# Column totals and a bank of inverses in the cross stage of a decoder layer

## The reference, cut to what matters

```python
sn = rmsnorm(slots, slot_norm_w)
scores = einsum('bkd,bmd->bkm', sn @ Wq.T, k_proj) * SCALE
attn = softmax(scores, axis=-2)                      # over the slots k
attn = attn / (sum(attn, axis=-1, keepdims=True) + EPS)   # over the context rows m
updates = einsum('bkm,bmd->bkd', attn, v_proj)
slots = gru_cell(updates, slots, ...)                # gates r, z and candidate n
```

## Time and profile before

| | |
|---|---|
| median of three runs | 669.06 us |
| span of the profiled execution | 664.9 us |
| what lies around the span (median less span) | 4.2 us |
| TensorE busy over the span | 621.7 us (93%) |
| VectorE busy | 493.7 us (74%) |
| ScalarE, GpSimd busy | 327.0 us (49%), 225.2 us (34%) |
| the four pairs in the cross stage, from the first `inputs` of one to that of the next | 82.8, 82.2, 82.3 us |

### The profile page before, as it was taken

The page is one execution under the profiler, slowest core; times in us unless marked ns, Lnnn a source line. Parts: engine busy times, 40 slices in busy tenths (PEclk is TensorE's granted clock), DMA queues, the critical chain, the costliest instruction groups (busy, mean ns, idle before and its releaser), DMA issues.

```text
span 664.9 us, 13964 instructions
## 1 busy us (share of the span) xinstructions
PE 621.7 (93%) x5064; PEld 565.3 (85%) x5064; DVE 493.7 (74%) x1039; ACT 327.0 (49%) x734; POOL 225.2 (34%) x274
## 2 busy tenths in 40 slices
PE   5988998998999999999999999999999998899996
PEld 4766787776767989999899998999989988799996
DVE  4755474674764788879888799887999888767653
ACT  5444553553575355655556555565566644231320
POOL 9402332432453251422223232232312213352543
PEclk9799898997999999999999999999999999999999
DMA  8634646357400040010000000000000000042240
GB/s 283 203 103 146 173 135 190 93 173 217 121 18 1 1 160 0 2 33 2 0 0 0 32 0 0 0 0 0 0 1 1 1 1 1 16 147 82 80 157 34
DMA packets 31374, 43.34 MB, mean 65 GB/s; under 512 B 3072, under 2 KB 18912, under 8 KB 31328
## 3 DMA queue, kind: packets, MB, share of 16 engines
q1 hardware_dynamic: 31328, 42.73, 21.1%
HBM read 29.39 MB, written 13.21 MB: 64 GB/s over the span
## 4 chain that ended last, share of the span: by engine, by line
PE 56%; DVE 13%; issue 13%; DMA 5%; SPq 5%; POOL 4%; ACT 3%; DVEq 0%; POOLq 0%; ACTq 0%
PE bank L448 26%; PE bank L2171 11%; PE bank L1991 4%; POOL hid_hl L801 3%; DMA k_rows<-k_hl 3%; PE bank L1891 2%; DMA q_op<-negT 2%; PE bank L1977 1%; PE bank L456 1%; PE bank L1849 1%; PE bank L2008 1%; SPq L519 1%; PE bank L1856 1%; PE bank L1872 1%; PE bank L2000 1%
## 5 line engine op out<-in xcount | busy, mean ns | idle before, releaser
L448 PE MATMUL bank<-slots_hl,whhT_hl 128*128 128x256 f32 x864 | 113.1, 284 | 0.0
L448 PEld LDWEIGHTS bank<-slots_hl,whhT_hl 128*128 128x128 f32 x864 | 105.5, 188 | 2.4 <-ACT gate_z L1104 1.0
L1293 DVE TENSOR_REDUCE neg_max<-bank 128x2 f32<-128x512 f32 (+1 forms) x96 | 65.7, 690 | 55.2 <-PE bank L1858 41.3
L2171 PE MATMUL bank<-attn_hl,vg_hl 128*128 128x256 f32 x864 | 105.7, 280 | 0.1
L2171 PEld LDWEIGHTS bank<-attn_hl,vg_hl 128*128 128x128 f32 x864 | 100.9, 188 | 4.3 <-ACT attn_hl L815 3.9
L870 ACT ACTIVATE pT<-bank 128x512 f32<-128x512 f32 x96 | 56.9, 598 | 57.7 <-PE bank L1872 41.7
L682 POOL TENSOR_SCALAR_AFFINE_SELECT pT<-pT 128x512 f32<-128x512 f32 x64 | 40.6, 638 | 117.5 <-ACT pT L870 117.4
L696 POOL TENSOR_TENSOR sq<-sq 128x256 f32<-128x256 f32 x24 | 18.1, 754 | 170.6 <-ACT sq L1089 130.3
L801 POOL TENSOR_TENSOR hid_hl<-hid,hid_hl 128x512 fp32r<-128x512 f32 x32 | 40.9, 1303 | 25.8 <-ACT hid_hl L815 25.7
L448 PE MATMUL bank<-x2T_hl,keys_hl 128*128 128x256 f32 x384 | 48.6, 284 | 0.0
L448 PE MATMUL bank<-values_hl,hid_hl 128*128 128x256 f32 x384 | 47.8, 281 | 0.3 <-DVE x L1567 0.3
(11 more groups left out here) (212 smaller groups left out, 1298.2 us busy)
## 6 DMA issues: line engine op xcount, KB each, us to landing
gate_rows<-gate_mem SPq DMA_DIRECT2D x48, 128.0 KB, 3.1
q_rows<-q_hl SPq DMA_DIRECT2D x21, 256.0 KB
k_rows<-k_hl SPq DMA_DIRECT2D x21, 256.0 KB
q_op<-q_rows SPq DMA_DIRECT2D x28, 192.0 KB, 3.2
k_op<-k_rows SPq DMA_DIRECT2D x14, 384.0 KB, 4.4
x_in<-in_x_dram SPq DMA_DIRECT2D x8, 256.0 KB, 6.6
c_in<-in_ctx_dram SPq DMA_DIRECT2D x8, 256.0 KB, 4.8
out_dram<-y_out SPq DMA_DIRECT2D x8, 256.0 KB, 2.8
```

The costliest lines, as they stand in the source:

```text
L448: mm = pe.matmul(dst, left(a), right(b), start=first and n == 0, stop=last and n == 2, skip_group_check=True)
L1293: dve.tensor_reduce(dst, src, AX.X, ALU.max, negate=True).then_inc(max_ok, 1)
L2171: mm = pe.matmul(halves(b)[:, m, :], vg_hl[:, j, v_part, 3 * t + r, q:q + P], attn_hl[:, j, at_part, t, :], start=n == 2 and a + m + t == ...
```

## The change

TensorE's `totals` now takes `tot` as the stationary operand, in two halves, and one column of 1/256 as the moving one: 256 totals come out as 128 x 2, slots on the partitions. VectorE scales and inverts those 128 x 2 elements; this stands between the second step of the gate (L1664) and the new slots, no longer behind them. A new step of TensorE, `inverse_totals`, spreads the two columns over a bank by two transposes of 128 x 128, and `weights` reads that bank. In a unit it stands between the state's parts for z and n; at a pair's end it stands between the first and second group of values. The `ib` job shares bank 2 with `tt` and is freed by `weights`. `weights` on VectorE now stands ahead of the mean square. On ACT, `attn_hi` and `hidden_out` stand ahead of the context's squares and of the expert weights' high parts, and the squares of the two contexts are made in units 2 and 3 instead of both in 3.

```diff
@@ ACT, cross
-                    if u == 3 and not last:
-                        context_squares(i, 0)
-                        context_squares(i, 1)
+                    if u == 4 and not last:
+                        context_text_hi(i, 0)
+                    if u + 1 < UNITS:
+                        attn_hi(i, u + 1)
+                    if u < 5:
+                        hidden_out(i, u + 1)
+                    if u in (2, 3) and not last:
+                        context_squares(i, u - 2)
                     if last and u < 4:
...
-                    if u < 4:
-                        hidden_out(i, u + 1)
-                    if u == 4 and not last:
-                        context_text_hi(i, 0)
-                    if u + 1 < UNITS:
-                        attn_hi(i, u + 1)
-                    if u == 4:
-                        hidden_out(i, u + 1)
@@ VectorE
             def totals(i, u):
                 dve.wait_ge(tt_mm, due(UNITS, i, u + 1))
-                dve.tensor_scalar(tot[:, :], bank[2][:, 0:T], float(D), RMS_EPS, ALU.mult, ALU.add).then_inc(tt_ok, 1)
+                dve.tensor_scalar(tot_col[:, :], bank[2][:, 0:NT], float(D), RMS_EPS, ALU.mult, ALU.add).then_inc(tt_ok, 1)
                 dve.wait_ge(tt_ok, due(UNITS, i, u + 1))
-                dve.reciprocal(inv_tot[:, :], tot[:, :]).then_inc(it_ok, 1)
+                dve.reciprocal(inv_col[:, :], tot_col[:, :]).then_inc(it_ok, 1)

             def weights(i, u):
                 j = u % 2
-                dve.wait_ge(it_ok, due(UNITS, i, u + 1))
-                dve.tensor_tensor(attn[:, j, 0, :], attn[:, j, 0, :], inv_tot[:, :], ALU.mult)
-                dve.scalar_tensor_tensor(attn[:, j, 1, :], attn[:, j, 1, :], s_inv[:, j, 1:2], inv_tot[:, :],
+                dve.wait_ge(ib_mm, due(UNITS, i, u + 1))
+                dve.tensor_tensor(attn[:, j, 0, :], attn[:, j, 0, :], bank[2][:, 0:T], ALU.mult)
+                dve.scalar_tensor_tensor(attn[:, j, 1, :], attn[:, j, 1, :], s_inv[:, j, 1:2], bank[2][:, 0:T],
                                          ALU.mult, ALU.mult).then_inc(at_ok, 1)
...
                     dve.wait_ge(cross_chain, i * CROSS_LINKS + next_link())
+                    if u + 1 < UNITS:
+                        totals(i, u + 1)
                     dve.scalar_tensor_tensor(slots[:, j, :, :], diff[:, :, :], 0.5, cand[:, :, :], ALU.mult, ALU.add).then_inc(sl_ok, 1)
...
                     if u + 1 < UNITS:
-                        totals(i, u + 1)
+                        weights(i, u + 1)
                     if u + 2 < UNITS:
                         mean_square(i, u + 2, 0)
-                    if u + 1 < UNITS:
-                        weights(i, u + 1)
@@ TensorE
                 pe.wait_ge(z_ok, due(UNITS, i, u + 1))
-                pe.matmul(bank[b][:, 0:T], mean_col[:, :].to_broadcast([P, P]), tot[:, :], start=True, stop=True).then_inc(tt_mm, 1)
+                for t in range(NT):
+                    mm = pe.matmul(bank[b][:, t:t + 1], tot[:, t * P:(t + 1) * P], mean_col[:, :], start=True, stop=True)
+                mm.then_inc(tt_mm, 1)
+
+            def inverse_totals(i, u, first=False):
+                b = free_bank(i, ("ib", u), first)
+                pe.wait_ge(it_ok, due(UNITS, i, u + 1))
+                for t in range(NT):
+                    mm = pe.transpose(bank[b][:, t * P:(t + 1) * P], inv_col[:, t:t + 1].to_broadcast([P, P]), ident[:, :])
+                mm.then_inc(ib_mm, 1)
...
                         totals(i, u + 1)
-                        state(i, u + 1, ("z", "hn"))
+                        state(i, u + 1, ("z",))
+                        inverse_totals(i, u + 1)
+                        state(i, u + 1, ("hn",))
...
                     totals(i, UNITS)
-                    context_values(i, 1)
+                    context_values_of(i, 1, 0)
+                    inverse_totals(i, UNITS)
+                    context_values_of(i, 1, 1)
+                    context_values_of(i, 1, 2)
```

More of the change, by code:

```diff
@@ L234, in decoder_layer @@
         tot = sb("tot", [P, T], where=s2)
-        inv_tot = sb("inv_tot", [P, T], where=s2)
+        tot_col = sb("tot_col", [P, NT], where=s2)
+        inv_col = sb("inv_col", [P, NT], where=s2)
         cand = sb("cand", [P, NC, T], where=s2)
@@ L295, in decoder_layer @@
         tt_mm, tt_ok, it_ok = event("tt_mm", UNITS), event("tt_ok", UNITS), event("it_ok", UNITS)
+        ib_mm = event("ib_mm", UNITS)
         at_ok, at_hi, at_lo = event("at_ok", UNITS), event("at_hi", UNITS), event("at_lo", UNITS)
@@ L379, in mid @@
         def mid(u):
-            return [(("tt", u), 2, tt_ok, UNITS, u + 1), (("r", u), 4, r_ok, UNITS, u + 1), (("z", u), 5, zt_ok, UNITS, u + 1),
+            return [(("tt", u), 2, tt_ok, UNITS, u + 1), (("ib", u), 2, at_ok, UNITS, u + 1), (("r", u), 4, r_ok, UNITS, u + 1), (("z", u), 5, zt_ok, UNITS, u + 1),
                     (("hn", u), 6, hb_ok, UNITS, u + 1)]
@@ L393, in decoder_layer @@
             jobs2 += front(UNITS)[:1] + context(0)[1:] + context(1)[:1] if u == 4 else []
-        jobs2 += context(1)[1:2] + mid(UNITS)[:1] + context(1)[2:] + [(("uT", 0), 2, x2_ok, 2, 1)] + front(UNITS + 1)[:1]
-        jobs2 += mid(UNITS)[1:] + [(("uT", 1), 0, x2_ok, 2, 2)]
+        jobs2 += context(1)[1:2] + mid(UNITS)[:2] + context(1)[2:] + [(("uT", 0), 2, x2_ok, 2, 1)] + front(UNITS + 1)[:1]
+        jobs2 += mid(UNITS)[2:] + [(("uT", 1), 0, x2_ok, 2, 2)]
         BANK2 = {job[0]: job[1] for job in jobs2}
@@ L407, in decoder_layer @@
                       ("ss", UNITS + 1): (2, rb_ok, due(UNITS, -1, UNITS + 1)), ("tt", UNITS): (2, ms_ok, due(UNITS, -1, UNITS + 2)),
+                      ("ib", UNITS): (2, it_ok, due(UNITS, -1, UNITS + 1)),
                       ("r", UNITS): (4, a_ok, 2 * B - 1), ("z", UNITS): (5, a_ok, 2 * B), ("hn", UNITS): (6, x1T_ok, B - 1)}
@@ L2054, in first_context @@
                     context_values_of(-1, 1, 2, True)
+                    inverse_totals(-1, UNITS, True)
             def project_first(b, batch, which):
```

## The result

The changed kernel takes 677.41 us (median of four runs, 675.87 to 685.06) where the kernel before, run beside it, takes 668.40 (four runs, 666.93 to 669.28): a ratio of 1.0173, interval 1.0132 to 1.0214. The medians differ by 9.0 us, and the ratio stands for some 11.6; 678.8 was predicted, in a range that holds the result. Sign and sum came out; several terms of the sum did not, and their errors partly cancel.

The account below looks back on a forecast made before the run. TensorE was taken to bound the first three pairs. Start +0.2, ordinary units 0, pair ends +8.3, last pair -0.6, last `inputs` -1.6 and clock +3.4 made +9.7 on 669.06: 678.8 us, range 674.0 to 683.5.

Parts of the forecast that it names:

- The end of a pair: Three pair ends: TensorE stands 3.05 us before the inverses, 3.06 us more each; less 0.5 taken back, 8.3 us in all.
- The clock: Behind the pair-end stalls: granted clock falls to 0.50 at two of three ends, 1.7 us each, +3.4 us.
- The ordinary unit: Ten steps from `inputs` to `inputs` in the first three pairs: sum 0.03, between -0.2 and +0.3, taken as 0.
- Slots 0.27 later: Ordinary unit, VectorE: scaling and reciprocal ahead of `slots` delay it, ScalarE's squares and POOL's sum by 0.27 us.
- the 0.24 wait for the high part: Ordinary unit, TensorE before `inputs`: the wait for `attn`'s high part goes, giving back 0.24 us.
- rival C: `attn`'s low part blocks POOL's power, 0.5 us in each of 16 steps: +8, 686.8; chance 0.10 with lesser forms.
- Neither rival: Rivals stated before the experiments: VectorE's later `slots`, or the inverses' own cost on TensorE, lengthen the units; no chance given.
- The last pair: Three units of the last pair: between -0.6 and +0.1 us, taken as -0.2 each, -0.6 together.
- The first unit of a pair: First unit after a pair's end: 0.5 us of TensorE's 0.62 us wait for `tot` taken back, between 0 and 0.62.
- the last `inputs`: Before the last `inputs`: TensorE's 1.81 us wait for the residual goes, inverses take 0.20: -1.6 us.
- unit 4 to 5: Unit 5's own inverses, before the long context work, cost TensorE 0.20 us each time.
- The 4.2 us around the span: Time outside the profiled span of 664.9 us, added to reach the median base of 669.06.

Follow-up runs that it names:

- e1: Changed kernel with VectorE taking unit 6's totals inside unit 5's gate at a pair's end too, ahead of slots and residual: 671.86 us, ratio 1.0082.
- e5: e1 plus `weights` of unit 6 ahead of the residual on VectorE, freeing bank 2 early: 666.82 us, ratio 1.0006 against the kernel before.
- e2: Changed kernel with the low part of `attn` made on POOL behind the power in every unit but the first: 674.9 us, ratio 1.0121.
- e3: Changed kernel with VectorE making the new `slots` ahead of the two small steps on the totals: 675.32 us, ratio 1.0121.
- e9: Changed kernel with ScalarE's order put back as in the kernel before: 674.01 us, ratio 1.0080.
- e4: Changed kernel with TensorE's inverses ahead of the first group of values at a pair's end: 686.35 us, ratio 1.0276.
- e6: e5 and e2 together, so the low part of `attn` is on POOL as well: 661.19 us, ratio 0.9931.
- e10: e5 with ScalarE's order put back as in the kernel before: 661.32 us, ratio 0.9920.
- e7: Kernel before with ScalarE's part of the change alone (`attn_hi` and `hidden_out` earlier, squares in units 2 and 3): 676.66 us, ratio 1.0167.
- e8: The changed kernel run again without edits, beside the others: 679.77 us, ratio 1.0215.

## Why the prediction was right, and where its terms failed

**The end of a pair: right.** The order of VectorE's queue gave the stall: 2.88 us on the loads for 3.05 forecast, a step 2.84 us longer for 3.06. The chain is that of the earlier trace rows, `slots`, residual, keys and totals, with 3.49 us from the start of `slots` to that of the totals (3.53 before); the small reciprocal took 0.17 us for 0.15. e1 and e5 show that the wait is the cause and that `weights` behind the residual is the next one, hidden by the stall.

**The clock: the kind of event right, the number too high.** "Three of four says two of the three ends: +3.4 us" became one end and 1.5 us. Over all kernels with a stall of 2.7 to 3.2 us the clock fell behind 8 of 15 ends (1, 1, 2, 1 and 3 of three in the changed kernel, its repeat, e2, e3 and e9), with 4.2 to 4.3 us behind 3 of 3 (e4), and behind none of e1, e5, e6 and e10. One half would have been nearer than three of four, on few cases. What decides between two ends with the same stall stays open.

**The ordinary unit: the step that failed.** "The low part of `attn` (L1231) comes close behind the mean square and may hold it in the same way, so of this 0.19 us I count nothing", and "I take 0 for the ten." Measured +0.25 each, +2.4. Slots 0.27 later and the 0.24 wait for the high part gone were right. The power did not stay at 0.89 us; it took a median of 1.15, that is +0.26, and 0.27 - 0.24 + 0.26 = +0.29. The event is that of rival C, but C's price of +0.5 was counted wrong: it set 1.39 us after the mean square against 0.89, and 0.89 is the power's own length, which starts 0.49 us behind the mean square's start (349.49 to 349.98). Counted from that start the power ended after 1.38 us before; held for a whole low part of 0.69 us it would have ended after 0.08 + 0.69 + 0.70 = 1.47. Measured is 1.65 (352.79 to 354.44), because the low part itself was lengthened to 1.01 us beside L784, which the prediction did not look at.

The other case is shown too: with the power at 0.70 the same sum is 0.27 - 0.24 - 0.19 = -0.16, or 11.14, and e9 measured 11.09 to 11.15 in the units where the high part is in time. e2, with the same power, stays 0.1 to 0.2 us above that, so the sum is no better than this. The source, which I had not followed, is ScalarE's new order. It makes the high part early, so the low part no longer waits and starts before the power. Neither rival explains the units alone: in e2 and e9 `slots` is as late and the inverses are there, and the units are at or below the length of before, but for e9's step from 3 to 4. The later `slots` is a term of the sum all the same: in e3, without it, 0.16 us came back.

The Trainium skill, SBUF — State Buffer, "Who interferes with whom", says that whoever issues first holds the shared port and the other waits for the whole instruction. The trace comes near to it where L1231 is first: the power gets on by some 0.14 us of its 0.70 in the 0.59 us beside it (1.15 - 0.59 = 0.56 come after). It is less strict in two other pairs: L1231 began 0.46 us before POOL's L784 ended and lost 0.32, and in e9 the low part began 0.24 us before the power ended and lost nothing.

**The last pair: sign wrong.** I took -0.2 each and measured +0.12 to +0.33. The reason is the collision again and ScalarE's order, and the two are only partly told apart: with the collision alone gone (e2) these units take 11.90, and in e10, without either, 11.52 to 11.53, the -0.3 that would have fitted. e7 shows how much that order alone can cost there (+1.1 each), where the old reciprocal makes `attn` late.

**Smaller terms.** The first unit of a pair gave 0.16 to 0.17 instead of 0.5; the last `inputs` 1.55 for 1.6, with no wait left before them; unit 4 to 5 0.15 to 0.18 for 0.20. The 4.2 us around the span were 1.7, and the profiled execution some 2.5 us quick; this shifted only the base.

**Why the total came out.** The repeat (e8) has 1.0215, and in the cross stage +11.5 was measured and +9.5 forecast: units +2.4, last pair +1.2 and first units +1.0 too little, the ends 2.6 too much (clock 1.9, stalls 0.7). Two things hid that difference. The base of 669.06, from three runs, lies 2.4 us above the 666.69 that 21 runs beside the repeat gave, and in the profiled pair the attention stage was 2.4 us shorter. So "slower", and the stall as its cause, were earned; the closeness of 677.4 to 678.8 was partly luck.

## What to carry to other kernels

When a small operation is put between two engines, read the queue that it stands behind at every place where it is issued, not only in the ordinary step: here three ends cost 10 us, moving the totals and `weights` forward on VectorE there (e5) took that back, and only without the collision in the units as well (e6, e10) did the cross stage become 3.6 and 5.0 us shorter than before. A step that is made earlier on one engine changes what runs beside what on the others; look for the pair that now starts in the other order. And one fall of the clock of the kind that a stall may bring is a chance to be priced as such, with kernels of the same stall showing one to three falls at three ends.

## What the runs showed of the hardware

POOL's power on 128 x 2 elements, busy for 0.70 us by itself, took 0.88 us (median) beside VectorE's `weights`, where it began in the middle of them, and 1.15 beside the low part, where that began 0.42 us earlier. In e3 the low part began only 0.16 us earlier, behind the end of L784 but for 0.04 us: the power took 1.08 and the low part kept 0.68. In e9 the power began first and shared its last 0.24 us, and both kept their length (0.70 and 0.69). Rows by line (minimum, median and maximum in ns), the power before and after and the low part after:

```profile
L706 POOL TENSOR_TENSOR s_rs<-s_ms,half_neg x24: 695/882/897, 219.6 to 527.4; 128x2 f32<-128x2 f32 x24
```

```profile
L709 POOL TENSOR_TENSOR s_rs<-s_ms,half_neg x24: 695/1146/1157, 217.0 to 538.0; 128x2 f32<-128x2 f32 x24
L1231 DVE TENSOR_TENSOR attn_hl<-attn,attn_hl x16: 944/948/1008, 242.4 to 537.7; 128x512 fp32r<-128x512 f32 x16
```

The kernel before took, over 22 runs beside the last experiments, 662.5 to 671.1 us. Between the profiles the cross stage of one kernel is the same to 0.01 us when as many falls of the clock lie in it (318.74 in both of the changed kernel), and the first `inputs` starts between 228.6 and 236.5 us over all profiles. So much of this spread seems to lie in the attention stage, whose stretches at the low clock differ in place and number between most of the profiles.
